# A vision tower's second attention on fixed PSUM banks, and identity products ahead of three later waits

## The reference, cut to what matters

```python
h = tokenise(x)                                   # patches, two layer norms, class token, positions
h = h + decay_attention(layernorm(h))             # first attention, 12 heads of 16
h = h + gqa_and_moe(layernorm(h))                 # second attention, then 16 experts
h = h + ternary_attention(layernorm(h))           # third attention, 12 heads of 16
h = h + grouped_experts(layernorm(h))             # second router, 8 experts and a shared one

# inside gqa_and_moe:
q, k, v = split(rms_norm(x) @ w_qkv)              # 12 query heads, 3 key/value heads, of 64
q, k = apply_rope(q), apply_rope(k)
attn = softmax(where(causal, q @ k.T / 8, min))   # per image and head
y = x + (attn @ v) @ w_out
return y + moe_ffn(rms_norm(y))                   # softmax router, two best of 16 experts

# inside ternary_attention: ternary weights, activations rounded to integers per token
attn = softmax(q @ k.T / 4)
return bitlinear(attn @ v, w_proj)
```

## Time and profile before

| | |
|---|---|
| median of three runs | 434.02 us (432.83 to 435.85) |
| profiled execution, its own time | 434.38 us |
| its span, first to last instruction | 432.6 us |
| busy in the span | PE 379.4 (88%), DVE 229.5 (53%), ACT 133.1 (31%), POOL 93.6 (22%) |
| mean granted TensorE clock | 0.964 of full |
| chain that ended last, shares | PE 65%, DVE 17%, ACT 6%, issue 6%, DMA 4% |
| identity products, L475 | 249, busy 61.4 us |

### The profile page before, as it was taken

How to read it: one execution, slowest core, us unless ns; L and a number is a source line. 1 busy time by engine, 2 the same in 40 slices (tenths; PEclk the granted TensorE clock), 3 DMA queues, 4 the chain that set the end, 5 groups by cost and what they waited for, 6 DMA issues and landing times.

```text
span 432.6 us, 7220 instructions
## 1 busy us (share of the span) xinstructions
PE 379.4 (88%) x2764; PEld 266.7 (62%) x2764; DVE 229.5 (53%) x658; ACT 133.1 (31%) x364; POOL 93.6 (22%) x104
## 2 busy tenths in 40 slices
PE   0387998899998999999699899959997988999996
PEld 0386555665455665785398789944546966656653
DVE  3826704668744444335344432225496786985664
ACT  0215332002225868220043233300227555311310
POOL 0402300014361434000335655420000000000000
PEclk9999999999999999997999999998997598999999
DMA  8970000008000000019349883118100000000000
GB/s 214 343 181 2 0 2 2 2 2 297 30 4 0 2 1 2 2 32 348 132 137 300 265 272 130 53 38 277 66 2 2 0 2 2 2 0 0 26 0 20
DMA packets 16472, 34.48 MB, mean 80 GB/s; under 512 B 3358, under 2 KB 8910, under 8 KB 16308
## 3 DMA queue, kind: packets, MB, share of 16 engines
q1 hardware_dynamic: 14554, 29.60, 21.6%
q0 software_dynamic: 1824, 4.36, 3.3%
q10 hardware_dynamic: 58, 0.03, 0.0%
HBM read 30.97 MB, written 3.13 MB: 79 GB/s over the span
## 4 chain that ended last, share of the span: by engine, by line
PE 65%; DVE 17%; ACT 6%; issue 6%; DMA 4%; POOL 1%; SPq 0%; DVEq 0%; POOLq 0%; ACTq 0%
PE slot L385 7%; PE slot L475 6%; PE slot L680 5%; PE slot L628 5%; PE slot L389 4%; PE slot L369 4%; PE slot L694 4%; PE slot L686 3%; PE slot L413 3%; ACT area_e L1127 3%; PE slot L574 3%; PE slot L511 2%; DVE nmax L1473 2%; DMA area_c<-xs_dram,area_d 2%; PE slot L553 2%
## 5 line engine op out<-in xcount | busy, mean ns | idle before, releaser
L475 PE MATMUL slot<-ident_bf 128*128 128x512 bf16 x249 | 61.4, 397 | 5.4 <-issue 4.3
L954 POOL TENSOR_TENSOR rstd<-var_eps,half_neg 111x3 f32<-111x3 f32 x20 | 17.3, 869 | 196.5 <-DVE var_eps L1332 111.1
L475 PEld LDWEIGHTS slot<-ident_bf 128*128 128x128 bf16 x249 | 24.0, 101 | 33.5 <-issue 9.2
L1653 DVE TENSOR_TENSOR area_c<-area_c,slot 128x384 f32<-128x384 f32 x19 | 10.5, 554 | 50.2 <-ACT area_c L1195 41.7
L1040 POOL DMA_INDIRECT ys_dram<-area_c,area_d x19 | 21.7, 1145 | 31.9 <-DVE area_c L1662 31.9
L1127 ACT ACTIVATE area_e<-slot,nmax 111x111 f32<-111x111 f32 x72 | 24.2, 376 | 9.6 <-DVE nmax L1473 9.6
L1473 DVE TENSOR_REDUCE nmax<-slot 111x6 f32<-111x666 f32 (+2 forms) x24 | 19.7, 843 | 10.9 <-PE slot L762 6.1
L553 PE MATMUL slot<-consts_sb,area_e 111*111 111x111 f32 x144 | 20.8, 306 | 4.5 <-ACT area_e L1249 3.4
L1025 POOL DMA_INDIRECT area_c<-xs_dram,area_d x19 | 18.6, 981 | 23.6 <-DVE area_d L1587 18.1
L553 PEld LDWEIGHTS slot<-consts_sb,area_e 111*111 111x111 f32 x144 | 19.3, 216 | 6.6 <-issue 2.5
L628 PE MATMUL slot<-area_b,area_w 128*111 128x192 f32 (+1 forms) x108 | 23.0, 342 | 0.1
(11 more groups left out here) (257 smaller groups left out, 764.1 us busy)
## 6 DMA issues: line engine op xcount, KB each, us to landing
area_e<-w_gate_up SPq DMA_DIRECT2D x10, 576.0 KB, 4.8
area_a<-w_gate_up SPq DMA_DIRECT2D x9, 576.0 KB, 4.3
area_w<-w_down SPq DMA_DIRECT2D x13, 288.0 KB, 6.1
area_a<-patches SPq DMA_DIRECT2D x6, 336.0 KB, 5.6
area_e<-w_down SPq DMA_DIRECT2D x6, 288.0 KB, 7.4
area_a<-w SPq DMA_DIRECT2D x1, 1728.0 KB, 9.6
area_c<-ys_dram SPq DMA_DIRECT2D x4, 252.0 KB, 4.4
w_tern_sb<-w_tern SPq DMA_DIRECT2D x1, 864.0 KB, 12.3
```

Source lines behind the costliest of these rows:

```text
L475: mm(bank, ident_bf[:], ident_bf[:].unsqueeze(1).to_broadcast([128, 4, 128]), start=True, stop=True)
```

## The change

The second attention leaves the ring. Each part has its own place: the eight first scores of every tile in `psum[0]`, the four last scores in the first bank of `psum[1]` and the four turned heads in its second bank, the eight turned heads in `psum[2]`, the attend in `psum[3]`. Each use waits for the reader of the same part one tile earlier. The last scores of a tile, which used two banks, now use one, in two halves of two heads with the eight transposes of the tile before between them (a new semaphore, `half_scored`). The identity products of this stage go from 47 to 19: 1 and 12 in tile 0, 6 in tile 1, none later. After the stage the ring starts again at `psum[0]`. Further, `keep_warm(7)` stands ahead of `turn_probs(TILES, 0)`, `keep_warm(5)` ahead of `turn_probs(TILES, 5)`, and `keep_warm(3)` ahead of `router_logits1(0)`. ACT and DVE keep their order and read from the new places.

```diff
-            def masked_scores2(t):
...
+            left = [list(freed) for freed in ring["freed"]]
+
+            def free_before(n):
+                for s, value in left[n]:
+                    pe.wait_ge(S[s], value)
+                left[n] = []
...
+            def first_scores2(t):
+                free_before(0)
+                if t:
+                    pe.wait_ge(S["probs"], 2 * t - 1)
+                for half in range(2):
+                    mask2(psum[0][:, half])
+                for i in range(REP):
+                    for half in range(2):
+                        last = masked_score2(t, psum[0][:, half], i, i, 6, half)
+                last.then_inc(S["score_done"], 1)
+
+            def last_scores2(t, half):
+                if half == 0:
+                    free_before(1)
+                    if t:
+                        pe.wait_ge(S["probs"], 2 * t)
+                    mask2(psum[1][:, 0])
+                else:
+                    pe.wait_ge(S["half_scored"], t + 1)
+                for i in range(2):
+                    last = masked_score2(t, psum[1][:, 0], 2 * half + i, 4 + i, 7, half)
+                last.then_inc(S["score_done" if half else "half_scored"], 1)
+
+            def turn_probs2(t, u):
+                free_before(2 - u)
+                pe.wait_ge(S["probs_scaled"], 2 * t + u + 1)
+                if t:
+                    pe.wait_ge(S[("probs_t_kept0", "probs_t_kept1")[u]], t)
...
             def attend2(t):
                 pe.wait_ge(S["probs_t_kept0"], t + 1)
                 pe.wait_ge(S["probs_t_kept1"], t + 1)
-                slot = take(pe, ("attend2", t), ("o2_t_ready", t + 1))
+                free_before(3)
+                if t:
+                    pe.wait_ge(S["o2_t_ready"], t)
+                slot = psum[3]
...
             for t in range(TILES):
                 pe.wait_ge(S["qk2_rotated"], 4 * (t // GROUP) + 4)
                 pe.wait_ge(S["v2_copied"], t // GROUP + 1)
-                if t == 2:
-                    keep_warm(10, slot_of[("probs_t", 0, 1)][:, 1, :])
-                masked_scores2(t)
+                first_scores2(t)
+                last_scores2(t, 0)
+                if t == 0:
+                    free_before(2)
+                    keep_warm(1, psum[2][:, 0])
+                else:
+                    turn_probs2(t - 1, 0)
+                last_scores2(t, 1)
+                if t == 0:
+                    keep_warm(12, psum[2][:, 0])
                 if t >= 1:
-                    if t == 1:
-                        keep_warm(5)
-                    else:
-                        keep_warm(4, slot_of[("probs_t", t - 2, 1)][:, 1, :])
-                    turn_probs(0, t - 1)
+                    turn_probs2(t - 1, 1)
+                if t == 1:
+                    free_before(3)
+                    keep_warm(6, psum[3][:, 0])
                 if t >= 2:
-                    keep_warm(4, slot_of[("probs_t", t - 1, 1)][:, 1, :])
                     attend2(t - 2)
...
+            ring["uses"] += -ring["uses"] % RING
+            ring["freed"] = [[("probs", 2 * TILES - 1)], [("probs", 2 * TILES), ("probs_t_kept1", TILES)],
+                             [("probs_t_kept0", TILES)], [("o2_t_ready", TILES)]]
             project_out2(0)
-            turn_probs(0, TILES - 1)
+            turn_probs2(TILES - 1, 0)
+            turn_probs2(TILES - 1, 1)
             attend2(TILES - 2)
             attend2(TILES - 1)
...
             scores3(1)
+            keep_warm(7)
             turn_probs(TILES, 0)
...
             attend3(4)
+            keep_warm(5)
             turn_probs(TILES, 5)
...
             turn_back3(5)
+            keep_warm(3)
             router_logits1(0)
```

More of the change, by code:

```diff
@@ L527, in _ @@
             pe.wait_ge(S["masks_made"], 1)
-            def masked_scores2(t):
-                for u, heads in enumerate((REP, 2)):
-                    slot = take(pe, ("score2", t, u), ("probs", 2 * t + u + 1))
-                    for b in range(2):
-                        mm(slot[0:ROWS, b, 0:heads * ROWS], ident_bf[0:ROWS, 0:ROWS],
-                           on_tiles(causal_bf[:], heads), start=True, stop=False, skip_group_check=True)
-                    for i in range(heads):
-                        for b in range(2):
-                            q, k = (i, 6) if u == 0 else (4 + i, 7)
-                            r = 64 * b
-                            last = mm(slot[0:ROWS, b, i * ROWS:(i + 1) * ROWS], qk2[r:r + 64, q, tile_cols(t)],
-                                      qk2[r:r + 64, k, tile_cols(t)], start=False, stop=True, skip_group_check=True)
-                    last.then_inc(S["score_done"], 1)
+            left = [list(freed) for freed in ring["freed"]]
@@ new lines, in free_before, with masked_score2, mask2 @@
+            def free_before(n):
+                for s, value in left[n]:
+                    pe.wait_ge(S[s], value)
+                left[n] = []
+            def masked_score2(t, bank, i, q, k, half):
+                r = 64 * half
+                return mm(bank[0:ROWS, i * ROWS:(i + 1) * ROWS], qk2[r:r + 64, q, tile_cols(t)], qk2[r:r + 64, k, tile_cols(t)],
+                          start=False, stop=True, skip_group_check=True)
+            def mask2(bank):
+                mm(bank[0:ROWS, 0:REP * ROWS], ident_bf[0:ROWS, 0:ROWS], on_tiles(causal_bf[:], REP), start=True, stop=False,
+                   skip_group_check=True)
@@ new lines, in turn_probs2 @@
+            def turn_probs2(t, u):
[3 more added lines that the diff above has]
+                    pe.wait_ge(S[("probs_t_kept0", "probs_t_kept1")[u]], t)
+                for i in range((8, 4)[u]):
+                    bank = psum[2][:, i // 4] if u == 0 else psum[1][:, 1]
+                    last = tr(bank[0:ROWS, (i % 4) * ROWS:(i % 4 + 1) * ROWS], p_buf[:, t % PB, 8 * u + i, :],
+                              ident[0:ROWS, 0:ROWS])
+                last.then_inc(S["probs_turned"], 1)
@@ L1135, in turned_probs @@
                     act.wait_ge(S["attended"], n - PB + 1)
-                fn(pt_buf[:, n % PB, 8:12, :], slot_of[("probs_t", n, 1)][0:ROWS, 0, 0:4 * ROWS].rearrange(
-                    "p (i x) -> p i x", x=ROWS), ACT.Copy).then_inc(S["probs_t_kept1"], 1)
+                bank = psum[1][:, 1] if n < TILES else slot_of[("probs_t", n, 1)][:, 0]
+                fn(pt_buf[:, n % PB, 8:12, :], bank[0:ROWS, 0:4 * ROWS].rearrange("p (i x) -> p i x", x=ROWS), ACT.Copy).then_inc(S["probs_t_kept1"], 1)
             def columns2(t):
@@ L1142, in columns2 @@
                     heads = 4 - 2 * b
-                    last = fn(o2_t[:, c, tile_cols(t)], slot_of[("attend2", t)][:, b, 0:heads * ROWS].rearrange(
+                    last = fn(o2_t[:, c, tile_cols(t)], psum[3][:, b, 0:heads * ROWS].rearrange(
                         "p (i n) -> p i n", n=ROWS), ACT.Copy)
@@ L1490, in _ @@
                 for u, per in enumerate((4, 2)):
-                    src = slot_of[("score2", t, u)][0:ROWS, :, 0:per * ROWS].rearrange("p b (i x) -> p b i x", x=ROWS)
+                    src = (psum[0][0:ROWS, :, 0:4 * ROWS].rearrange("p b (i x) -> p b i x", x=ROWS) if u == 0 else
+                           psum[1][0:ROWS, 0, 0:4 * ROWS].rearrange("p (b i x) -> p b i x", b=2, x=ROWS))
                     negative_max(t, u, src, per).then_inc(S["nmax_ready"], 1)
```

13 lines of the change are left out of this document (5 added, 8 removed).

## The result

The changed kernel takes 422.03 us (median of four runs, 420.01 to 426.95), the kernel before 433.42 in the same comparison (431.01 to 435.85). The ratio is 0.972, with a 95% interval from 0.966 to 0.978: faster, by 11.4 us at the medians.

A forecast was written before the change was run, and what follows sets the result against it. The second attention was bound by a ring of waits including the attend, the third by TensorE at a halved clock. 434.38 - 4.5 - 4.5 - 0.5 + 0.3 = 425.2, stated as 425.0 us; range 422.5 to 430.

The forecast's parts named there:

- The step that failed: Between second and third attention: router, expert loads and expert blocks shift with the second attention, with no gain of their own.
- Second attention: Loop on fixed banks: turn falls from 6.97 to 5.63 us, last attend gives 0.7 back; -4.5 us (-2.5 to -5.2).
- TensorE's own work: Second attention, per turn: 6.78 us less eight products, plus up to 0.5 for halves, 4.7 to 5.2, below the turn.
- the ring of exponentials: Second attention: exponentials, mask and scores, maximum, next exponentials, without the attend's 1.34, set a turn of 5.63 us.
- the last scores in two halves: Second attention: the last scores run as two halves at different times in one bank, allowed up to 0.5 us of TensorE.
- the eight products: Second attention: two batches of four identity products filling waits, no longer run; 2.1 us less TensorE work per turn.
- Third attention: Seven identity products before the first transposes hold the clock, third turn-back at 343.8, not 348.34: -4.5 us (0 to -6.8).
- the first rival: Third attention: the clock falls anyway, halfway (2.3 of the 4.5 left) or at once (none); 427.3 to 429.6 us, chance 0.22.
- Five products ahead of the last transposes: Third attention: overrun of 0.2 to 0.3 us hidden, dip at 360.4 to 363.7 spared; 0.5 us gain (0 to 0.9).
- The three ahead of the logits: Before the second router's logits: 0.7 us of identity products in a 0.36 wait, 0.3 us lost.
- The clock falling in the loop: Second attention: TensorE at the lower level takes 9.9 us per tile; two tiles 433.6 us, four 442; chance 0.08.
- The "better" rival: First router: no clock fall at its logits saves 1.1 us, up to 1.8 with products ahead; 423.2 us, chance 0.10.

The follow-up runs named there:

- the run with 140 waits: Changed kernel plus 140 already-met waits (70 instructions) early in TensorE's list, moving the jump back to where the kernel before has it: 426.54 us, ratio to before 0.987.
- better version: Changed kernel with the last attend in psum[2] and four more identity products ahead of tile 2's transposes in the third attention: 419.38 us against 424.24, 0.966 of before.

## Why the forecast came out too high

**The step that failed** is "What follows (router, expert loads, expert blocks) is released by this work and shifts with it". Nothing between the second and third attention was edited, but its code was moved, and the jump there lost 3.1 us of its idle time (4.07 in the mean of the long traces with 78 products, 0.97 of the short ones). With the clock held and the integers no longer late, 1.35 more went from the stretch behind it (36.9 to 35.6 in the means). Together **-4.4**, a term that the sum did not have. Had the jump stayed in its place, the change would have been worth 6.1 us and not 9 (the run with 140 waits against its own before; more by whatever those waits cost). The kernel before showed the idle time, as "issue" in its chain of waits:

```profile
286.02 1.26 PE slot L694 x6
287.28 0.02 issue
287.30 0.37 DVE area_c L1662
287.67 3.90 issue
291.57 18.70 PE slot L475 x78
```

I read the chain only where the diff was. Nor did I read the clock's dip of slice 27, which the forecast names and leaves: it is the fall behind this idle time, 0.61 in 291.57 to 296.00 above.

**Second attention: -4.0, not -4.5.** The mechanism was as forecast: attend out of the ring, ScalarE idle 0.51 per turn (forecast 0.4), first projection 4.7 earlier (5.2), last attend waiting 0.98 (0.7). The term that was mis-sized is TensorE's own work. I put it at 5.2 at most and let the ring of exponentials, 5.63, set the turn; it took 5.75 and became the bound. Allowing 0.5 for the last scores in two halves was nearly right (two of 0.57 for one of 0.57, from 152.62 to 153.19 in the earlier trace rows). That the transposes would be split too was left out. And the eight products were taken off at 2.1. TensorE's timeline before, beside the earlier trace rows:

```profile
148.28 1.03 PE L475 MATMUL slot<-ident_bf 128*128 128x512 bf16 x4
...
155.24 1.03 PE L475 MATMUL slot<-ident_bf 128*128 128x512 bf16 x4
```

Counted from start to start, twelve transposes took 1.17 in one go (154.07 to 155.24) and now take 0.96 + 0.57 = 1.53, and the eight products held TensorE for 0.88 (153.19 to 154.07) and 1.03, which is 1.9. These three are the difference between 5.2 and 5.75, within 0.1.

**Third attention: -2.7 in the mean, -4.0 at best, not -4.5.** The clock held in seven of the ten traces with the seven products, and there the stretch took 16.20 each time. In three it fell midway, as the first rival said, and 17.54, 17.79 and 18.38 were left, against 19.4 in the mean of the five traces without the products (16.7 is the mean of the ten). The forecast took the likeliest case whole, and its sum holds nothing of the rival; which of the two comes is a matter of each execution. Where the clock held, the transposes were followed by the third turn-back after 14.47, where the forecast's steps make 13.9 (343.8 - 329.91). Of these 0.6, 0.5 were gone when VectorE began its first pass, 2.37 behind the transposes' start at 325.82 and not 1.33 + 0.57 = 1.9:

```profile
328.19 0.85 DVE L1521 TENSOR_REDUCE nmax<-slot 111x6 f32<-111x666 f32 x1 [1.14 <-PE slot L808]
```

**The small terms.** Five products ahead of the last transposes: no effect where the clock held anyway (17.65 from third turn-back to logits with them, 17.64 without). The dip that they were to spare shows as 18.5 in two traces of five without them and in none of ten with them; that makes 0.4 in the mean, near the forecast's 0.5, but from few traces. The three ahead of the logits cost 0.12, not 0.3, and with them the clock mostly held behind the logits (above), which the forecast did not count.

**Rivals.** The clock falling in the loop did not come: 1.00 in every turn. When I provoked the fall, it cost 3.3 and lasted a turn and a half, less than the 8.6 at which the forecast put two tiles. The Trainium skill's statement ("TensorE: Matmul & The Clock Gate", Part 4 on PE-mode transpose) that a transpose does not count as busy work in the same way, taken as the forecast took it, spoke for a clock that stays down there. With 1.53 us of transposes in each turn of 5.75 and no products behind tile 0 the trace shows it come back and stay at 1.00, so here the measurement decides against that consequence. The "better" rival was underpriced. The clock falls in the first router in some executions and not in others, in old and new kernels alike (the second group's logits, changed kernel and better version, against the earlier trace rows):

```profile
193.52 2.83 PE L369 MATMUL slot<-wr_sb,x_t 128*111 128x16 f32 x12
```

```profile
187.80 1.84 PE L369 MATMUL slot<-wr_sb,x_t 128*111 128x16 f32 x12
```

Without the fall the stretch to the first expert product takes 30.0 to 30.2, with it 32.3 to 33.8: 2.2 us and more, where I had 1.1 to 1.8.

**The balance.** -4.0, -4.4 and -2.7 make -11.1, where the medians differ by 11.4. That it fits so well is partly luck: stretches that no edit touches, such as the start and the experts, differ by several us between executions. And of the -2.7 the whole times show only a part: 1.2 with the products alone (at most 3.0 by its interval), and 1.3 between the changed kernel without them (423.23) and with them (421.91). The forecast's last step has a slip of its own: 425.2 less the 0.36 is 424.8, not 425.0.

## What to carry to other kernels

Read "issue" in the chain of waits over the whole program, and ask at every jump what the engine waits for: an edit that only changes the number of instructions ahead of it can win or lose some microseconds, and a run with idle waits put in at the start tells that apart from the edit's own worth. Identity products in a wait are free only while they end before the data they wait for; behind anything that may be late they pass the delay on, so their count is to be set by the time at which the data come. And a price for a clock that holds "or falls" is better taken as a mean over executions.

## What the runs showed of the hardware

- Idle time behind a jump that skips code: 0.95 to 0.98 us or 3.9 to 4.3 us, by the place of the jump in the engine's list, the same again after a shift of about 256 instructions, with a 16 KB packet of the instruction queue inside the long one and none in the short one.
- The granted clock can also fall where TensorE is busy all the time: in three of the ten traces with all or some of the new products it dropped to about 0.5 for some 3 us, 40 us behind the second router's first logits and 3 us behind the start of those of its second group, in windows with 3.00 busy of 3.00 and after 10 us as busy. No run explains it.
- A wait of 0.84 us ahead of the transposes of tile 2 was followed by a fall of the clock within 2 us in three of nine traces, and by none in the other six.
